# A two-layer graph network on one core: TensorE gets six products on constants behind each pair of build products of the first layer

## The chip, the cores and the metric

The kernel runs on 1 core of one Trainium2 chip. The metric is device time in microseconds (us); lower is better. Three runs of the kernel before took 5845.89, 5846.42 and 5848.63 us, median 5846.42 us.

## What is computed

There are 12500 nodes with 32 features and 400000 edges, sorted by destination. The first layer gathers the source's row for each edge, adds the edge's features, takes the relu and sums over each destination; then comes a layer norm with a residual. The second layer gathers, sums and scales by the square roots of both degrees, and there is a second layer norm. Cut to what matters:

```python
def _L0_gnn_ref(node_feat, edge_feat, eps, src, dst):
    m = jax.nn.relu(node_feat[src] + edge_feat)
    neigh = jax.ops.segment_sum(m, dst, num_segments=node_feat.shape[0])
    return (1.0 + eps[0]) * node_feat + neigh

def _L1_gnn_ref(node_f, src, dst):
    out_deg = jnp.clip(jax.ops.segment_sum(ones, src, num_segments=n), 1.0)
    in_deg = jnp.clip(jax.ops.segment_sum(ones, dst, num_segments=n), 1.0)
    x = node_f * jax.lax.rsqrt(out_deg)[:, None]
    agg = jax.ops.segment_sum(x[src], dst, num_segments=n)
    return agg * jax.lax.rsqrt(in_deg)[:, None]

x = _layernorm(x + _L0_gnn_ref(x, edge_attr_32, L0_gnn_eps, src, dst), axis=-1)
x = _layernorm(x + _L1_gnn_ref(x, src, dst), axis=-1)
```

## The kernel before

The edges are cut into G = 125 groups of 3200 edges (128 partitions x J = 25). The first layer (`layer_0`) handles one group per **turn**. The function `turns` writes turns 0 to 3 out, runs turns 4 to 119 in a loop of 29 passes with four turns each, and writes out turns 120 to 126. Each engine has its own program of `step(g, slot, u)`, and semaphores alone tie them together.

- **GpSimd (POOL)** issues the 25 row gathers of turn g (L166), into one of four buffers `rows`. Ahead of the first it waits until the sums of step g - 1 are done:

```python
gp.wait_ge(z_agg, g - 1)
gathers(gp, 0, J, x[:, :], rows[:, slot, :, :], src_t[:, slot, :], z_rows[slot])
```

- **VectorE (DVE)** works one turn behind. In step g it waits for the rows of turn g - 1 and adds them to the edge features (`add(0)`, L427), makes the parts of `msg` and the one-hot matrix `hot`, takes the sums of the step before out of PSUM (`sums_out`, L467 and L468), and makes one-hot matrices `b_hot` and `key_hot` for the build products, in three chunks a turn.
- **TensorE (PE)** makes two kinds of products in step g. The **build products** (L708) are 12 pairs, n = 0 to 11, into the two PSUM buffers `built[n % 2]`; they count edges per pair of nodes, and the second layer uses the counts. The **sums** (`sum_up`, L688) are 25 products of `msg` with `hot` into one bank; they aggregate the messages of turn g - 1. Three sums stand behind pair 9, three behind pair 10 and 19 behind pair 11; the last one raises `z_agg`. A small product (`fold_sums`, L676) stands ahead of pair 8. Pair n waits until ScalarE has copied pair n - 2 out of PSUM.
- **ScalarE (ACT)** copies each pair to `stage`, a part of the tile `big` (`evict`, L642). Between these copies stand its six steps on messages, L620, L627 and L631. The copy of pair 1 stands behind `first_part(0)` (L627), which waits for `add(0)`.
- **SyncE (SP)** loads indices and edge features, and stores `stage` to memory once a turn.

`spare` in the change is the identity matrix `ident`, 128x128 in float32, seen as 128x256 numbers in bf16. `fold_bank` is the PSUM bank of L676, which uses its partitions 0 to 32; the new products write its partitions 64 to 127.

The second layer (`layer_1`) follows behind a barrier. It has no gathers in its main loop: it applies the stored counts with products of 160 columns (L1082).

Of the kernel before, what the change touches and what calls it, by code (L numbers as in the profile page):

```python
# [4 lines left out]
F32, BF16, F16, I32, U32 = mybir.dt.float32, mybir.dt.bfloat16, mybir.dt.float16, mybir.dt.int32, mybir.dt.uint32  # L5
# [4 lines left out]
P = 128  # L10
# [6 lines left out]
def build(nc, x, src, dst, edge, eps, out, table, x1):  # L17
# [47 lines left out]
    with ExitStack() as ctx:  # L65
# [15 lines left out]
        ident = sb("ident", [P, P])  # L81
# [11 lines left out]
        A1 = 64  # L93
# [128 lines left out]
        def layer_0():  # L222
# [5 lines left out]
            def turns(engine, step):  # L228
                for g in range(4):
                    step(g, g, 0)  # L230
                with engine.Fori(0, fours) as i:
                    for slot in range(4):
                        step(i * 4 + (4 + slot), slot, i + 1)
                for g in range(4 + 4 * fours, G + 2):
                    step(g, g % 4, g // 4)

            def builds(g):

                return not isinstance(g, int) or g < G

            def sends(g):

                return not isinstance(g, int) or 1 <= g <= G

            def adds(g):

                return not isinstance(g, int) or 2 <= g
# [12 lines left out]
            with ExitStack() as own:  # L260
# [112 lines left out]
                def prepare_pe(te):  # L373
                    te.wait_ge(s_v, n_first)
                    PE(te.transpose(misc[0:JT, 0:NC], c_first[:, :], ident[0:NC, 0:NC]))
                    te.wait_ge(s_v, n_keys)
                    for k, (what, t, m) in enumerate(ROUNDS):
                        if k >= 2:
                            te.wait_ge(s_a, k - 1)
                        for q in range(m):  # L380
                            turned = (c_hi, c_key)[what][:, t + q, :]
                            last = te.transpose(turn[k % 2][0:TP, q * NC:(q + 1) * NC], turned, ident[0:NC, 0:NC])
                        PE(last)
                    te.wait_ge(s_v, n_base)
                    PE(te.matmul(spread[:, 0:G], ones_row[:, :], first[0:1, :], start=True, stop=True))
                    te.wait_ge(s_v, n_bad)
                    for h in range(2):
                        te.matmul(misc[0:HS[h], h * NC:(h + 1) * NC], pick[:, h, 0:HS[h]], first[:, :], start=True, stop=True)
                    PE(te.matmul(misc[0:1, 2 * NC:2 * NC + 1], bad[:, :], ones[0:NC, :], start=True, stop=True))
# [8 lines left out]
                with nc.Block() as block:  # L398
# [266 lines left out]
                    @block.tensor  # L665
                    def _(te):
                        te.wait_ge(s_v, n_const)
                        prepare_pe(te)

                        def step(g, slot, u):  # L670
                            def fold_sums():

                                if adds(g):

                                    te.wait_ge(z_taken, g - 1)
                                    te.matmul(folded, fold_r[:, :], taken[:, :], start=True, stop=True).then_inc(z_folded, 1)  # L676

                            def sum_up(j0, j1):

                                if not sends(g):  # L680
                                    return
                                for j in range(j0, j1):
                                    if j == 0:

                                        te.wait_ge(z_hot, g)
                                    if j == JA:
                                        te.wait_ge(z_part2[1], g)
                                    last = te.matmul(agg_bank[:, :], msg[:, j, :], hot[:, j, :], start=(j == 0), stop=(j == J - 1))  # L688
                                if j1 == J:
                                    last.then_inc(z_agg, 1)  # L690

                            if not builds(g):
                                fold_sums()
                                sum_up(0, J)
                                return
                            for n in range(BP):
                                if n == 2 * CP:
                                    fold_sums()
                                r = (slot * HB + n // CP) % 2
                                if n % CP == 0:  # L700
                                    te.wait_ge(z_chunk[n // CP], g + 1)
                                if n >= 2:
                                    te.wait_ge(z_counts[n - 2], g + 1)
                                elif not (isinstance(g, int) and g == 0):
                                    te.wait_ge(z_counts[BP + n - 2], g)
                                for b in range(2):
                                    t = n % CP * 2 + b
                                    last = te.matmul(built[n % 2][:, b, 0:KEYS], b_hot[:, r, t, :], key_hot[:, r, t, :], start=True, stop=True)  # L708
                                last.then_inc(z_built[n], 1)
                                if n >= BP - 3:  # L710

                                    sum_up((n - BP + 3) * 3, (n - BP + 4) * 3)
                            sum_up(9, J)
                        turns(te, step)

                general_sums(0, x[:, :], J, DE, (src_t, dst_t, rows, quot, hot[:, :, 0:W], agg_bank[:, 0:W]), edge_t, msg[:, :, X:R], msg[:, :, 0:1])
# [643 lines left out]
```

## Time and profile before

| | value |
|---|---|
| median of three runs | 5846.42 us |
| span of the profiled execution, first to last instruction | 5163.0 us |
| its own time | not given beside its span; the median less the span is 683.4 us |
| first layer, first gather to last sum | 9.3 us to about 3936 us |
| second layer, from there to the end | about 1227 us |
| mean granted TensorE clock over the span | 0.735 |

### The profile page before, as it was taken

The numbers are of one execution on the slowest core, as the hardware profiler recorded it, in microseconds if no ns is written. First come the engines' busy times: TensorE is split into PE (matmuls) and PEld (weight loads), VectorE is DVE, ScalarE is ACT, GpSimd is POOL, SyncE is SP. The second block draws the span as 40 slices with busy tenths as digits, with TensorE's granted clock in tenths as the row PEclk, the third lists the DMA queues.
The fourth block names the chain that finished last, engine by engine and source line by source line (L and its number), as shares of the span: only waits on it lengthen the run. The fifth ranks groups of instructions, "written<-read, shape, count | busy, mean of one in ns | idle before, by whom it ended". The sixth has DMA issues, their size and how long they took to land. (4 is left out here: it accounts for less than half of the span.)

```text
span 5163.0 us, 62751 instructions
## 1 busy us (share of the span) xinstructions
PE 3304.6 (64%) x21148; PEld 1672.0 (32%) x21148; DVE 3278.0 (63%) x4723; ACT 2748.4 (53%) x2907; POOL 2960.2 (57%) x3134
## 2 busy tenths in 40 slices
PE   4555555555555555555555555555555999999998
PEld 1111111111111111111111111111113888888887
DVE  7766666666666666666666666666666444444444
ACT  4555555555555555555555555555554555555554
POOL 7777777777777777777777777777772000000000
PEclk8666666666666666666666666666666999999998
DMA  3333333333333333333333333333334999999996
GB/s 126 120 120 134 129 120 120 120 120 126 126 134 123 120 120 120 120 122 135 126 120 120 120 121 126 128 134 120 120 117 168 327 328 326 326 326 326 327 327 232
DMA packets 269133, 867.70 MB, mean 168 GB/s; under 512 B 90218, under 2 KB 140218, under 8 KB 252602
## 3 DMA queue, kind: packets, MB, share of 16 engines
q1 hardware_dynamic: 169107, 815.98, 42.5%
q0 software_dynamic: 100000, 51.40, 6.1%
q8 instruction: 13, 0.21, 0.0%
q14 instruction: 13, 0.11, 0.0%
HBM read 486.77 MB, written 380.38 MB: 168 GB/s over the span
## 5 line engine op out<-in xcount | busy, mean ns | idle before, releaser
L166 POOL DMA_INDIRECT rows<-in_x,src_t x3125 | 2958.5, 947 | 959.1 <-issue 946.9
L708 PE MATMUL built<-x_parts,b_hot 100*128 100x490 bf16 x3000 | 1289.6, 533 | 1757.8 <-ACT big L642 1743.4
L642 ACT ACTIVATE big<-built 128x980 bf16<-128x980 f32 x1500 | 1803.2, 1228 | 542.7 <-PE built L708 539.1
L708 PEld LDWEIGHTS built<-x_parts,b_hot 100*128 100x128 bf16 x3000 | 248.8, 111 | 2644.1 <-ACT big L642 2025.7
L1082 PE MATMUL applied<-counts,x_parts 128*96 128x160 bf16 x12250 | 915.9, 233 | 18.1 <-DVE x_parts L894 18.1
L427 DVE TENSOR_TENSOR sum_ps<-sum_ps,rows 128x416 f32<-128x416 f32 x250 | 142.9, 572 | 1210.9 <-DMA rows<-in_x,src_t 1205.7
L688 PE MATMUL agg<-hot,msg 128*128 128x512 bf16 x3125 | 899.2, 438 | 11.4 <-DVE msg L457 11.4
L1082 PEld LDWEIGHTS applied<-counts,x_parts 128*96 128x96 bf16 x12250 | 880.0, 123 | 79.4 <-issue 19.4
L146 DVE TENSOR_TENSOR x_parts<-iota_ps,hk_g 100x3920 bf16<-100x3920 f16 x375 | 819.4, 2185 | 0.0
L1038 ACT ACTIVATE counts<-built 128x980 bf16<-128x980 f32 x496 | 594.7, 1240 | 386.8 <-PE built L1065 386.8
L146 DVE TENSOR_TENSOR hot<-iota_ps,s_hi 128x5252 bf16<-128x5252 f16 x250 | 691.3, 2765 | 0.0
L627 ACT ACTIVATE msg<-sum_ps 128x416 bf16<-128x416 f32 x250 | 122.8, 491 | 793.6 <-DVE sum_ps L427 793.6
L688 PEld LDWEIGHTS agg<-hot,msg 128*128 128x128 bf16 x3125 | 351.1, 112 | 511.9 <-issue 240.6
L631 ACT ACTIVATE msg<-sum_ps 128x416 bf16<-128x416 f32 x250 | 125.9, 504 | 383.7 <-DVE sum_ps L432 383.7
L146 DVE TENSOR_TENSOR big<-iota_ps,hk_g 100x3920 bf16<-100x3920 f16 x125 | 273.6, 2189 | 0.0
L1065 PE MATMUL built<-big,hi_hot 100*128 100x490 bf16 x992 | 269.0, 372 | 0.8 <-DVE big L146 0.8
L146 DVE TENSOR_TENSOR b_hot<-iota_ps,hk_g 100x1024 bf16<-100x1024 f16 x375 | 255.1, 680 | 7.9 <-PE built L708 3.6
L1005 DVE CAST slots<-small 80x64 bf16<-80x64 f32 x125 | 27.6, 221 | 355.0 <-PE small L1093 355.0
L146 DVE TENSOR_TENSOR hot<-iota_ps,rel 128x1404 bf16<-128x1404 f16 x250 | 209.7, 839 | 0.0
L620 ACT ACTIVATE sum_ps<-edge_t 128x416 f32<-128x416 f32 x250 | 126.9, 508 | 68.6 <-DVE msg L436 68.6
L1019 DVE TENSOR_TENSOR acc<-acc,small 32x108 f32 x125 | 33.2, 266 | 200.0 <-PE small L1103 200.0
L432 DVE SCALAR_TENSOR_TENSOR sum_ps<-sum_ps,msg 128x416 f32<-128x416 f32 x250 | 141.5, 566 | 3.7 <-ACT msg L627 3.7
(132 smaller groups left out, 1425.0 us busy)
## 6 DMA issues: line engine op xcount, KB each, us to landing
stash<-big SPq DMA_DIRECT2D x125, 2940.0 KB
counts<-stash SPq DMA_DIRECT2D x250, 1470.0 KB, 8.7
rows<-in_x,src_t POOLq DMA_INDIRECT x3125
edge_t<-in_edge_attr SPq DMA_DIRECT2D x61, 800.0 KB
big<-in_dst SPq DMA_DIRECT2D x1, 1562.5 KB
big<-in_src SPq DMA_DIRECT2D x1, 1562.5 KB
src_t<-in_src SPq DMA_DIRECT2D x61, 24.8 KB
dst_t<-in_dst SPq DMA_DIRECT2D x61, 24.8 KB
```

Source lines behind the costliest of these rows:

```text
L146: return ve.tensor_tensor(out.rearrange("p n (w t) -> p n w t", t=2), row[0:p, 0:w].rearrange("p (w t) -> p w t", t=2).unsqueeze(1).to_bro ...
L166: gp.indirect_dma_start(rows_d[:, j, :], None, nodes, bass.IndirectOffsetOnAxis(ap=src_d[:, j:j + 1].bitcast(U32), axis=0),).then_inc(s, 16)
L427: ve.tensor_tensor(half(h), half(h), rows[:, prev, j0:j1, :], ALU.add).then_inc(z_sum[h], 1)
L432: ve.scalar_tensor_tensor(half(h), half(h), 0.0, part(0, h), ALU.max, ALU.subtract).then_inc(z_left[h], 1)
L620: sc.activation(half(h), edge_t[:, prev, j0:j1, :], ACT.Copy).then_inc(z_copy[h], 1)
L631: sc.activation(part(1, h), half(h), ACT.Copy).then_inc(z_part1[h], 1)
L642: sc.activation(stage[:, slot % 2, q, :, d0:d0 + 2 * SPAN].rearrange("p c (b d) -> p b c d", b=2), built[n % 2][:, :, 0:KEYS].rearrange("p ...
L688: last = te.matmul(agg_bank[:, :], msg[:, j, :], hot[:, j, :], start=(j == 0), stop=(j == J - 1))
L708: last = te.matmul(built[n % 2][:, b, 0:KEYS], b_hot[:, r, t, :], key_hot[:, r, t, :], start=True, stop=True)
L1038: sc.activation(counts[:, slot, HB, :, d0:d0 + 2 * SPAN].rearrange("p c (b d) -> p b c d", b=2), built[n % 2][:, :, 0:KEYS].rearrange("p b ...
L1065: last = te.matmul(built[n % 2][:, b, 0:KEYS], hi_hot[:, slot, t, :], key_hot[:, slot, t, :], start=True, stop=True)
L1082: last = te.matmul(applied[slot].rearrange("m (q d) -> m q d", d=CS), x_parts[:, c, :], counts[:, other, :, c, :], start=(c == 0), stop=(c ...
```

## The change

TensorE's program of the first layer gets a helper that makes n products of the same constants, 64 output partitions by 256 columns. It is called with n = 6 behind each of the 12 pairs of build products of a turn, and behind the last sum. Nothing reads the result, and nothing waits for these products but what stands behind them in TensorE's own program.

```diff
                         prepare_pe(te)
 
+                        spare = ident[:, :].bitcast(BF16)
+
+                        def idle_products(n):
+                            for _ in range(n):
+                                te.matmul(fold_bank[A1:P, 0:256], spare[:, 0:P - A1], spare[:, :], start=True, stop=True)
+
...
                                 if j1 == J:
                                     last.then_inc(z_agg, 1)
+                                    idle_products(6)
...
                                 last.then_inc(z_built[n], 1)
+                                idle_products(6)
                                 if n >= BP - 3:
 
                                     sum_up((n - BP + 3) * 3, (n - BP + 4) * 3)
```

The first place is the end of a turn on TensorE, inside the loop. These are the rows of the kernel before, from the build products of pairs 8 and 9 to the 19 last sums:

```order
L708 MATMUL built<-x_parts,b_hot 128x490 x4
L688 MATMUL agg<-hot,msg 128x512 x3
L708 MATMUL built<-x_parts,b_hot 128x490 x2
L688 MATMUL agg<-hot,msg 128x512 x3
L708 MATMUL built<-x_parts,b_hot 128x490 x2
L688 MATMUL agg<-hot,msg 128x512 x19
```

The same stretch in the changed kernel, where L715 is the build product, L674 the new one and L694 the sum:

```order
L715 MATMUL built<-x_parts,b_hot 128x490 x2
L674 MATMUL fold_bank<-ident 64x256 x6
L715 MATMUL built<-x_parts,b_hot 128x490 x2
L674 MATMUL fold_bank<-ident 64x256 x6
L694 MATMUL agg<-hot,msg 128x512 x3
L715 MATMUL built<-x_parts,b_hot 128x490 x2
L674 MATMUL fold_bank<-ident 64x256 x6
L694 MATMUL agg<-hot,msg 128x512 x3
L715 MATMUL built<-x_parts,b_hot 128x490 x2
L674 MATMUL fold_bank<-ident 64x256 x6
L694 MATMUL agg<-hot,msg 128x512 x19
L674 MATMUL fold_bank<-ident 64x256 x6
```

Of the new products of a turn, 18 stand between the pairs 9 to 11 and the sums that follow them, six stand behind the last sum, and the other 54 stand behind the pairs 0 to 8. No other row of TensorE moves, and the programs of the other engines are unchanged.

## Rows read from the trace of the kernel before

**Rows 1.** The page: busy tenths, clock and DMA in 40 slices of the span.

```profile
POOL 7777777777777777777777777777772000000000
PEclk8666666666666666666666666666666999999998
```

**Rows 2.** Groups of instructions between 2000 and 3000 us (busy, mean; idle before).

```profile
L166 POOL DMA_INDIRECT rows<-in_x,src_t x801 | 755.9, 944 | 244.1 <-issue 242.9 <-PE agg L688 1.2
L642 ACT ACTIVATE big<-built 128x980 bf16<-128x980 f32 x385 | 462.9, 1228 | 138.8 <-PE built L708 138.2
```

**Rows 3.** Who waited for whom between 2000 and 3000 us: total, times, longest.

```profile
PE built L708 <- ACT big L642: 457.4, 192, 8.2
DVE sum_ps L427 <- DMA rows<-in_x,src_t: 320.1, 32, 10.4
```

**Rows 4.** The waits of POOL between 0 and 260 us.

```profile
POOL rows L166 <- PE agg L688: 3.3, 2, 3.0
```

**Rows 5.** Timeline of POOL: the gather that waited, and the last turn's first and last.

```profile
146.15 0.94 POOL L166 DMA_INDIRECT rows<-in_x,src_t  x1 [2.96 <-PE agg L688]
...
3891.63 0.94 POOL L166 DMA_INDIRECT rows<-in_x,src_t  x1 [0.30 <-issue]
...
3921.59 0.94 POOL L166 DMA_INDIRECT rows<-in_x,src_t  x1 [0.30 <-issue]
```

**Rows 6.** Timeline of PE: sums of step 3, then pairs 3 to 11 and sums of step 123.

```profile
141.07 4.26 PE L688 MATMUL agg<-hot,msg 128*128 128x512 bf16 x19
...
3864.29 1.00 PE L708 MATMUL built<-x_parts,b_hot 100*128 100x490 bf16 x2 [7.29 <-ACT big L642]
3867.58 2.05 PE L708 MATMUL built<-x_parts,b_hot 100*128 100x490 bf16 x4 [2.29 <-ACT big L642]
...
3876.61 1.00 PE L708 MATMUL built<-x_parts,b_hot 100*128 100x490 bf16 x2 [2.09 <-ACT big L642]
3877.40 1.49 PE L688 MATMUL agg<-hot,msg 128*128 128x512 bf16 x3
3878.68 1.02 PE L708 MATMUL built<-x_parts,b_hot 100*128 100x490 bf16 x2
...
3881.34 4.26 PE L688 MATMUL agg<-hot,msg 128*128 128x512 bf16 x19
```

**Rows 7.** Windows: busy time of PE, PEld, DVE, ACT, POOL; clock; DMA share, GB/s.

```profile
61.40:75.00 13.60, 11.55 (x24) 1.71 (x24) 8.32 (x7) 12.38 (x11) 10.25 (x12) 0.50 0.10 13
3876.60:3881.00 4.40, 4.39 (x11) 1.63 (x12) 4.32 (x9) 3.44 (x3) 3.43 (x4) 0.50 0.10 15
3881.10:3891.20 10.10, 5.93 (x27) 2.36 (x25) 2.02 (x1) 2.94 (x3) 7.66 (x9) 1.00 0.77 304
3943.00:3955.00 12.00, 12.00 (x83) 9.41 (x82) 9.18 (x16) 3.48 (x3) 0.00 (x0) 0.50 0.10 11
```

**Rows 8.** Timeline of PE: transposes against the identity matrix, before the first turn.

```profile
45.05 3.33 PE L382 MATMUL built<-ident,x_parts 125*100 125x125 f32 x16 [22.50 <-DVE big L354]
48.55 1.14 PE L382 MATMUL built<-ident,x_parts 125*100 125x125 f32 x8 [0.17 <-ACT hk_all L607]
```

**Rows 9.** Timeline: products of 160 columns in the second layer; ACT in step 123.

```profile
4000.34 1.89 PE L1082 MATMUL applied<-counts,x_parts 128*96 128x160 bf16 x25
...
3875.29 3.55 ACT L642 ACTIVATE big<-built 128x980 bf16<-128x980 f32 x3
```

**Rows 10.** Timeline of all engines around the last rows' landing; then DVE in step 123.

```profile
3924.46 0.52 DVE L457 TENSOR_TENSOR msg<-iota_ps,s_lo 128x372 bf16<-128x372 f16 x1
3924.91 0.58 DVE L427 TENSOR_TENSOR sum_ps<-sum_ps,rows 128x416 f32<-128x416 f32 x1
...
3862.00 0.60 DVE L427 TENSOR_TENSOR sum_ps<-sum_ps,rows 128x416 f32<-128x416 f32 x1 [10.19 <-DMA rows<-in_x,src_t]
```

**Rows 11.** DMA queues that carry code, and two issues (KB each, us to landing).

```profile
q8 instruction: 13, 0.21, 0.0%
q14 instruction: 13, 0.11, 0.0%
...
counts<-stash SPq DMA_DIRECT2D x250, 1470.0 KB, 8.7
...
edge_t<-in_edge_attr SPq DMA_DIRECT2D x3, 400.0 KB, 3.4
```

## The prediction

> **What bounds the kernel now.** I read the page's slices first. In the first 30 of 40 slices POOL is steady at 7 tenths and TensorE's clock is 0.6; behind that POOL is nearly empty and the clock is near full [rows 1]. Seven tenths is not idle time: in the groups of a stretch of 1000 us, 801 gathers keep POOL busy for 755.9 us, and of the 244.1 us between them 242.9 are "issue", the 0.30 us that stand ahead of every gather whatever else happens [rows 2]. So a gather costs 1000/801 = 1.248 us and a turn 25 x 1.248 = 31.2 us. The timeline shows that this holds everywhere. Turn 4 begins at 146.15 and the last gather, the 3025th from there on, at 3921.59 [rows 5]: 3775.44 us for 3024 steps, 1.2485 us each. From 146 us on POOL waits for nobody, and the first layer lasts as long as its gathers.
>
> The waits show the reverse side. VectorE waits for rows in each of 32 turns, up to 10.4 us and 320.1 us in all, and TensorE waits 457.4 us in 1000 for ScalarE's copies [rows 3]. TensorE is late for nobody as long as `z_agg` comes before POOL needs it.
>
> How much room is there? In step 123 the last 19 sums start at 3881.34 and end at 3885.60 [rows 6]; the first gather that waits for them starts at 3891.63 [rows 5]. Where POOL really waited, the sums ended at 141.07 + 4.26 = 145.33 [rows 6] and the gather began at 146.15 [rows 5], 0.8 us later. So the room is 3891.63 - 0.8 - 3885.6 = 5.2 us. A delay beyond it is not paid whole. Gathers of turn g wait for the sums of step g - 1, and the sums of step g + 1 wait for those gathers, so the ring takes two turns: a delay of e behind the sums costs (e - 5.2)/2 a turn.
>
> **What the change costs on TensorE.** The trace has no product of 64x256. Sums of 512 columns follow each other at (3878.68 - 3877.40)/3 = 0.427 us at the low clock and 4.26/19 = 0.224 us at the high one [rows 6]; half the columns gives 0.213 and 0.11 us. From the other side, 25 products of 160 columns take 1.89 us at the high clock, 0.076 us each [rows 9]; by columns that is 0.12 us. I take 0.213 and 0.11: six cost 1.28 us low and 0.66 us high, and their weight loads lie under the product before, as those of the sums do. A pair of build products takes 0.79 us low (3877.40 - 3876.61) [rows 6], about 0.42 high. With its six it takes 2.07 or 1.08 us; ScalarE copies a pair in 3.55/3 = 1.18 us [rows 9]. At the high clock ScalarE stays the slower one, at the low clock TensorE becomes it. A turn's 78 new products are 16.6 us low or 8.6 us high.
>
> So all hangs on the clock. In the window from 3876.60 to 3881.00 TensorE was busy 4.39 of 4.40 us at 0.50, and in the next window it has 1.00 [rows 7]. From 61.40 to 75.00 it was busy only 11.55 of 13.60 us, with build products alone, and the clock stayed at 0.50 [rows 7]. With the new products it has no gap there.
>
> I walk step 123 with the clock rising some 4.4 us after the dense stretch begins. Pair 3 starts at 3864.29, as now, since it waits for rows. Pair 4 waits for its copy until 3867.58, ends with its six at 3869.7; pair 5 ends at 3871.8; there the clock is high. Pairs 6 and 7 end at 3872.9 and 3874.0, the fold and pair 8 at 3875.4. Pair 9 waits for the copy of pair 7 until 3876.6, as now. Then come three pairs with their sixes (3 x 1.08), six sums (1.3) and 19 sums (4.26): 3885.4 us, against 3885.6. The sums come when they came, and POOL notices nothing: **0 us** for turns 4 to 124. What is faster on TensorE is added to its idle time, and what is slower is taken from it.
>
> Beside the row stands the Trainium skill, page "TensorE: Matmul & The Clock Gate", section "Why this matters for your kernels": keep TensorE busy without a break, and the clock stays at its full rate. By that rule the sums and builds halve. By the groups above this still takes nothing from 1.2485 us a gather, so the sum by rule and row is the same, 0.
>
> **Where TensorE does stand on the path.** (a) The start. POOL's only long wait is 2.96 us for the sums of step 3 [rows 4, 5]; steps 0 to 3 run as fast as VectorE, ScalarE and TensorE allow, the gathers being ahead. In step 0 pair 1 comes 1.28 us late behind the first six at the low clock, later pairs keep ScalarE's pace. At the end of steps 1 to 3, six products stand ahead of pair 0 (0.66 us each); against that, the pairs that ScalarE waits for come up to 0.4 us earlier. Bounds: -2.7 us (the wait is gone, 2.96 less the usual 0.30) and 1.3 + 3 x 1.1 = +4.6 us; I take +2. (b) The end. In step 125 VectorE reaches the last rows at 3924.91, with L457 ending just then (3924.46 + 0.52) [rows 10], so sums of step 124 that come late push it; by the walk they come at -0.2, and I take 0 with a bound of +2. The six behind the last sum lie under VectorE's copy that the fold waits for. The second layer has none of the new products, and the 683.4 us outside the span stay. Sum: 5163.0 + 2 + 683.4, about 5848.4 us.
>
> **Rivals.** *1, the clock rises only with the sums.* The low clock isn't left for every busy stretch: from 3943 to 3955 narrow transposes kept TensorE busy 12.00 of 12.00 us at 0.50 [rows 7]. The new products use half the output partitions and operands that are nearly all zeros. For the rise speaks that transposes against the same identity matrix went from 3.33/16 = 0.208 to 1.14/8 = 0.143 us each within one burst [rows 8]. The Trainium skill has a rule against that in the same page, section "Part 4: PE-mode transpose": transposes don't count as busy for the gate; in this trace those of rows 8 did end in the high clock, the narrow ones didn't. In this case pair 9 begins at 3867.58 + 5 x 2.07 + 0.6 for the fold = 3878.5, and the clock rises 4.4 us behind that, at 3882.9. Pair 9 and three sums end at 3881.9, pair 10, partly at the high clock, at 3883.4, three sums and pair 11 at 3885.1, the 19 sums at 3889.4: 3.8 us late, inside the 5.2. The loop costs nothing, but the start does: step 0 runs 12 pairs at 2.07 instead of 1.18 (+10 us), and steps 1 to 3 lose 3 to 4 us each, like the 3.8 above. Together +12 to +25, about 5866 us. Chance 0.16.
>
> *2, the constants hold the clock down until the 19 sums, the case on the other side.* Pairs, sixes and the first six sums low: pair 9 begins at 3878.5, pair 11 with its six ends 3 x 2.07 + 6 x 0.427 later, at 3887.3. With a rise 4.4 us into the 19 sums (10 low, 9 high) these end at 3893.6: 8.0 us late, (8.0 - 5.2)/2 = 1.4 us a turn, 168 us over 120 turns; all low 9.8 us late, 276 us. With 25 to 30 us at the start: +193 to +306, about 6090 us. It decides from 5.2 us late on. It needs the clock not to answer to TensorE being full, which rows 7 and 8 speak against. Chance 0.08.
>
> *3, code.* The loop's four turns hold 4 x 50 = 200 products before and 4 x 128 = 512 now, each with a weight load. Before, neither code queue moved more than 13 packets for 29 passes [rows 11], so the loop was not fetched again. If a longer one is, the nearest landings are 3.4 and 8.7 us [rows 11]. Once a pass, at the branch behind the sums, this falls into 7 us of idle TensorE and costs 0; once a turn ahead of the sums, (8.7 - 5.2)/2 x 120 = 210 us at most. The Trainium skill, page "Runtime: NRT & Kernel Launch", section "Instruction fetch mechanics", says that a taken branch to code that is no longer held forces such a fetch, and gives TensorE's store as 2048 instructions; the new loop is by that an estimated 1050. Chance 0.04.
>
> *4, faster by over 0.2%* (11.7 us, about what a measurement can tell from no change): the gathers would have to get cheaper, and the start gives 2.7 us at most. Chance 0.03.
>
> **How the numbers follow.** My forecast, the clock high from early in each dense stretch, has 0.66 and its own range 5842 to 5856. With 1, 2, 3, 4 and 0.03 for what I don't see that is 1. The range 5841 to 5880 holds the forecast and rival 1, 0.82. Same: 0.66 and a fifth of rival 1 and half of 3, 0.71. Slower: the rest of 1, 2, half of 3, the unseen, 0.25. Faster: 0.04.
>
> **What would show it.** Right: POOL 801 gathers per 1000 us and no wait for L694 beyond 0.3; clock near 0.8 to 1.0 instead of 0.66 over the first layer; the six in about 1.3 and 0.66 us; ScalarE's waits for build products shorter; the gather of turn 4 between 143.5 and 151 us; as many code packets per pass as before, none. Wrong: the clock at 0.5 between 61 and 80 us and in pairs 3 to 9 (rival 1); POOL waiting 1.5 us or more per turn for the sums (2); code packets in the loop (3); or a time outside the span other than 683 us.

## The result, and the profile after

The changed kernel takes **7469.98 us** (four runs, 7464.41 to 7477.74) beside 5846.16 us (5844.13 to 5848.63): the ratio is 1.2778, with a 95% interval from 1.276 to 1.2796. It is 28% slower. The forecast was 5848.4 us.

The page of the changed kernel answers to [rows 1] and the table: the span, the slices of POOL and of the clock, and the costliest groups of POOL, ScalarE and the new products.

```profile
span 7463.6 us, 82126 instructions
...
POOL 5344454444544454444544454444544451000000
PEclk7777677766777667776777667766777677999999
...
L166 POOL DMA_INDIRECT rows<-in_x,src_t x3125 | 2957.5, 946 | 3238.0 <-PE agg L694 2318.3
L642 ACT ACTIVATE big<-built 128x980 bf16<-128x980 f32 x1500 | 1810.5, 1231 | 4072.3 <-remote 2567.9
```

Two things stand there. A gather costs what it cost (946 ns), but POOL now waits 2318.3 us in all for the sums, where it had waited 1.2 us in a stretch of 1000 [rows 2]. And the time less the span is 7465.73 - 7463.6 = 2.1 us for the profiled run, where for the kernel before I had 683.4 us.

The waits between 2000 and 3000 us answer to [rows 3]:

```profile
ACT big L642 <- remote: 463.5, 57, 17.1
...
POOL rows L166 <- PE agg L694: 368.5, 20, 19.2
PE built L715 <- ACT big L642: 304.4, 37, 16.3
```

POOL waits 18.4 us in each of 20 turns. ScalarE waits up to 17.1 us for something the profile calls "remote": it finds no instruction that ended just then. The timeline of one turn shows what that is. The last gather of the turn is at 2051.41, the next turn's first at 2070.38.

```profile
2021.44 0.95 POOL L166 DMA_INDIRECT rows<-in_x,src_t  x1 [18.78 <-PE agg L694]
...
2027.80 0.59 PE L715 MATMUL built<-x_parts,b_hot 100*128 100x490 bf16 x2
...
2029.92 0.59 PE L715 MATMUL built<-x_parts,b_hot 100*128 100x490 bf16 x2 [0.76 <-issue]
...
2037.18 1.19 ACT L642 ACTIVATE big<-built 128x980 bf16<-128x980 f32 x1 [6.93 <-remote]
...
2051.41 0.94 POOL L166 DMA_INDIRECT rows<-in_x,src_t  x1 [0.31 <-issue]
2054.74 1.19 ACT L642 ACTIVATE big<-built 128x980 bf16<-128x980 f32 x1 [16.04 <-remote]
...
2065.29 4.27 PE L694 MATMUL agg<-hot,msg 128*128 128x512 bf16 x19
...
2070.38 0.94 POOL L166 DMA_INDIRECT rows<-in_x,src_t  x1 [18.02 <-PE agg L694]
```

TensorE ends pair 5 at 2028.4 and pair 6 at 2030.5 (the two build rows). ScalarE copies pair 5 at 2037.18, after 6.93 us of idleness, and pair 6 at 2054.74, after 16.04 us. By the profile the work is done, but **the signal that it is done arrives 9 and 24 us late**. In this turn the second one comes 2.4 us after POOL's last gather ended (2051.41 + 0.94 = 2052.35). Only then does the turn go on: 15 us of pairs and sums until 2069.6, and the next gathers. So this turn is 30.9 us of gathers, 2.4 us, and 15.6 us of what should have run under them: 48.9 us instead of 31.2.

In the trace's records of semaphores, beside the modelled ends of the products that raise them, this reads as follows, in us. Some records are missing, so only products with one record each are told. The kernel before is here its trace ahead of the prediction, which is of another kind of chip, as the experiments will show.

```
product that signals        kernel before       changed kernel
pair 7, L708 / L715         0.014               0.014 to 22.8, median 19.1
fold, L676 / L682           0.014               0.014 to 22.3, median 18.2
last sum, L688 / L694       0.014               0.014
second layer's products     0.014               0.014
```

Three things stand in these records of the changed kernel. Only TensorE's signals are late: from the fifth turn to the 119th, 607 of its 1450 records lie over 0.3 us behind the work, and none of ScalarE's 1446 or VectorE's 1362 (of which three in ten are missing, though). Each turn begins on time: the signals of pairs 0 to 2 come after 0.014 us, though gathers are in flight. And a late signal isn't held until the gathers pause: over 108 turns, pair 5's 81 recorded signals all came while gathers still ran, and so did 38 of pair 6's 93. What was left came out after them: pair 7's and the fold's signals 4.5 and 4.6 us (medians) behind the end of the turn's last gather, every time.

The same trace holds the other half. POOL waits for the sums from about 143 to 243 us, so no gather is issued, and there steps 2 and 3 of the changed kernel run undisturbed: the 19 sums of steps 1, 2 and 3 start at 188.01, 213.81 and 238.04 us, 24 to 26 us apart, and the signals of the pairs come after 0.014 us.

```profile
243.12 0.94 POOL L166 DMA_INDIRECT rows<-in_x,src_t  x1 [99.97 <-PE agg L694]
```

### The profile page after: what moved, and what is told of

It is laid out like the page before. It is cut to its first block and busy times, and to the rows that moved or that the text cites. A ratio compares the mean times of both kernels' runs of the same rounds, so it can differ in the third digit from the quotient of the medians.

```text
span 7463.6 us, 82126 instructions
## 1 busy us (share of the span) xinstructions
PE 4427.6 (59%) x30773; PEld 2606.7 (35%) x30898; DVE 3333.9 (45%) x4723; ACT 2716.0 (36%) x2907; POOL 2959.2 (40%) x3134
## 5 line engine op out<-in xcount | busy, mean ns | idle before, releaser
L166 POOL DMA_INDIRECT rows<-in_x,src_t x3125 | 2957.5, 946 | 3238.0 <-PE agg L694 2318.3
L715 PE MATMUL built<-x_parts,b_hot 100*128 100x490 bf16 x3000 | 1060.2, 441 | 2891.2 <-ACT big L642 1750.2
L674 PE MATMUL fold_bank<-ident 128*64 128x256 bf16 x9750 | 1638.7, 313 | 0.0
L674 PEld LDWEIGHTS fold_bank<-ident 128*64 128x64 bf16 x9750 | 1063.8, 123 | 897.7 <-issue 835.9
L715 PEld LDWEIGHTS built<-x_parts,b_hot 100*128 100x128 bf16 x3000 | 206.6, 103 | 3301.3 <-issue 2530.8
L694 PE MATMUL agg<-hot,msg 128*128 128x512 bf16 x3000 | 757.3, 397 | 50.2 <-issue 38.8
L436 DVE TENSOR_TENSOR msg<-sum_ps,msg 128x416 bf16<-128x416 f32 x250 | 142.2, 569 | 1316.7 <-ACT msg L631 1019.9
L694 PEld LDWEIGHTS agg<-hot,msg 128*128 128x128 bf16 x3125 | 283.3, 101 | 414.6 <-issue 137.9
L521 DVE TENSOR_TENSOR acc<-acc,fold_bank 33x108 f32 x125 | 32.4, 259 | 416.0 <-remote 406.4
```

The source lines that it names most:

```text
L166: gp.indirect_dma_start(rows_d[:, j, :], None, nodes, bass.IndirectOffsetOnAxis(ap=src_d[:, j:j + 1].bitcast(U32), axis=0),).then_inc(s, 16)
L436: ve.tensor_tensor(part(2, h), half(h), part(1, h), ALU.subtract).then_inc(z_part2[h], 1)
L674: te.matmul(fold_bank[A1:P, 0:256], spare[:, 0:P - A1], spare[:, :], start=True, stop=True)
```

## The experiments

Each row of a run's record gives a time and a span; all differ by some 2 us. Chips are told apart by the kernel before on them: **5167 us (first kind, two chips)** or **5847 to 5854 us (second kind, three chips)**. The trace ahead of the prediction, with its span of 5163.0 us, is one of the first kind, and the three times beside it are of the second. Only one chip, of the first kind, was used on two occasions, so whether a kind belongs to the chip or to its condition at the time is not told apart; "kind of chip" stands for either.

| kernel | first kind, us | second kind, us |
|---|---|---|
| before | 5166.9, 5166.9, 5166.4 | 5846.9, 5846.8, 5848.1, 5853.75 |
| six products of 256 columns (the change) | 5176.5 | 7472.6, 7480.3 |
| three of 256 | 5178.9, 5178.4, 5180.2 | 6738.8 |
| three of 512 | 5171.8, 5172.2 | 7026.0 |
| six of 64 | 5176.6, 5176.6 | 7205.0 |
| six, behind the last sum alone | 5168.3 | |
| twelve of 256 | | 8393.0 |
| six of 256, no gathers | | 4368.5 |

All are single runs but 5853.75 (seven) and 7480.3 (four).

**Three products, sums alone, wide and narrow ones.** The edits of the first four runs, each against the changed kernel:

```diff
-                                    idle_products(6)
+                                    idle_products(3)
...
-                                idle_products(6)
+                                idle_products(3)
```

> Three constant products instead of six at each place. In the changed kernel the work of TensorE is done early, but what it signals to ScalarE (the end of a build pair) arrives up to 38 us late while gathers are in flight. Theory A (each product instruction issued while gathers are in flight adds to that lateness): about half of the added 1620 us, 6500 to 6800 us. Theory B (a threshold or a state of the whole run, not the number of products): near 7460 or near 5850 us, nothing between. Theory C (TensorE's time itself is on the path): 5850 us, because half of the time of six, 4.3 us a turn at the high clock, fits into the room.

For the sums alone the call behind the build pairs is taken out:

```diff
                                 last.then_inc(z_built[n], 1)
-                                idle_products(6)
```

> Only the six products behind the last sum of a turn stay; the 72 behind the build pairs are gone. Theory A: 6 of 78 products, about +125 us or less, 5850 to 5970 us. Theory B (state): 7460 or 5850 us. Theory C: 5846 us.

The wide ones: three calls instead of six, and

```diff
-te.matmul(fold_bank[A1:P, 0:256], spare[:, 0:P - A1], spare[:, :], start=True, stop=True)
+te.matmul(fold_bank[A1:P, 0:512].rearrange("p (a c) -> p a c", a=2), spare[:, 0:P - A1], spare[:, :].unsqueeze(1).to_broadcast([P, 2, 256]), start=True, stop=True)
```

> Three products of 512 columns instead of six of 256: TensorE's time is as in the changed kernel, the number of product instructions is half. Theory A (number of instructions): as with three products of 256 columns, 6500 to 6800 us. Theory C (TensorE's time or its activity): as in the changed kernel, about 7465 us.

The narrow ones:

```diff
-te.matmul(fold_bank[A1:P, 0:256], spare[:, 0:P - A1], spare[:, :], start=True, stop=True)
+te.matmul(fold_bank[A1:P, 0:64], spare[:, 0:P - A1], spare[:, 0:64], start=True, stop=True)
```

> Six products of 64 columns instead of 256: as many instructions as in the changed kernel, a quarter of the columns. Theory A (number of instructions): about 7465 us or more, since they come closer together. Theory C (TensorE's time or activity): 5850 to 6250 us.

Measured: 5178.93, 5168.26, 5171.76 and 5176.64 us, beside **5166.94 us for the kernel before**. None of the theories was tested, since the kernel before had lost its 680 us as well. That was the find: from one chip to another, a kernel that hasn't changed differs by 13%.

**The changed kernel again, and twelve products.** The second is the changed kernel with `idle_products(12)` in both places.

> The changed kernel once more, beside a kernel before that takes 5167 us on this chip and not 5846. Theory D (the 5846 and the 7470 us belong to a condition of the chip or session in which TensorE's signals are late while gathers are in flight, in both kernels): 5170 to 5200 us. Theory E (six products of 256 columns pass a threshold that three, or six narrow ones, do not pass): about 7465 us here too, beside 5167.

> Twelve products instead of six at each place: 156 a turn, 17.2 us at the high clock, so 28 us of TensorE's 31.2 us a turn are used. Theory D: TensorE's time decides, and the sums come some 4 us later than with six, 5180 to 5350 us. Theory E: above the changed kernel, 8500 us or more.

Measured: 7480.3 us beside 5853.75 us, ratio 1.278 (1.2758 to 1.2801), and 8393.01 us. This was another chip, of the second kind, so D and E weren't told apart yet. Twelve add 8393.0 - 7480.3 = 913 us to six, 7.5 us in each of 121 turns: less than theory E's 8500 us and far above theory D's 5350 us.

**The first four once more, for the other kind of chip.**

> The kernel before, for its trace on a chip where it takes about 5850 us. Theory D (late signals of TensorE while gathers are in flight, on some chips): there its build pairs of the middle of a turn are seen by ScalarE microseconds late, POOL waits for the sums some 5.5 us a turn, and 121 turns of 36.8 instead of 31.2 us make the 683 us. On a chip where it takes 5167 us: no such waits.

> Three products of 256 columns at each place, 39 a turn. On a chip where the kernel before takes 5167 us: 5179 us as measured. Where it takes about 5850 us: theory A (lateness grows with the number of product instructions) 6550 to 6800 us; theory C (with TensorE's time) the same.

> Three products of 512 columns, as many instructions as with three narrow ones and as much TensorE time as in the changed kernel. Chip at 5167: 5172 us. Chip at 5850: theory A as three products of 256 columns, 6550 to 6800 us; theory C about 7470 us.

> Six products of 64 columns, as many instructions as in the changed kernel and a quarter of the columns. Chip at 5167: 5177 us. Chip at 5850: theory A about 7470 us; theory C 6000 to 6300 us.

Measured: 5166.42, 5178.4, 5172.23 and 5176.55 us. It was the chip of the first four again; each repeats its first time within 0.6 us.

**The second kind of chip, with a trace of the kernel before, and without gathers.** The edit of the third run leaves the 3125 row gathers out and loads fixed rows, once a turn, so it computes something else:

```diff
-gathers(gp, 0, J, x[:, :], rows[:, slot, :, :], src_t[:, slot, :], z_rows[slot])
+gp.dma_start(rows[:, slot, :, :].rearrange("p j d -> p (j d)"),
+             x[0:P * J, :].rearrange("(p j) d -> p (j d)", p=P)).then_inc(z_rows[slot], 16)
...
-ve.wait_ge(z_rows[prev], loads(slot, u) * (16 * J))
+ve.wait_ge(z_rows[prev], loads(slot, u) * 16)
```

> The changed kernel a third time, so far only measured where the kernel before takes 5850 us. If this chip takes 5167 us for the kernel before: theory D (a condition of the chip) 5170 to 5200 us; theory E (a threshold of the kernel's own) about 7470 us. If it takes 5850 us: 7470 us, and the runs below are read against it.

> The kernel before, for its trace. Theory D, where it takes 5850 us: pairs of the middle of a turn seen late by ScalarE while gathers are in flight, POOL waiting about 5.5 us a turn for the sums, fewer records of gather landings. Where it takes 5167 us: 5166 us and no such waits, as before.

> The changed kernel without its 3125 row gathers; one plain transfer a turn brings fixed rows, so the result is not that of the reference. TensorE's work and the new products are unchanged. Theory D (lateness needs gathers in flight): turns of 22 to 26 us as between 160 and 250 us of the changed kernel's trace, 4100 to 4500 us on either chip. Theory F (the new products make TensorE's signals late whatever else runs): above 6000 us where the changed kernel takes 7470.

> Six products of 64 columns instead of 256. Chip at 5167: 5177 us. Chip at 5850: theory A (lateness grows with the number of product instructions) about 7470 us; theory C (with TensorE's time) 6000 to 6300 us.

Measured: 7472.58, 5848.07, 4368.48 and 7205.01 us. These four settle most. First the **kernel before** on this kind of chip. The waits of POOL over the whole span answer to [rows 4]:

```profile
POOL rows L166 <- issue: 915.6, 3003, 0.3
POOL rows L166 <- remote: 620.0, 120, 5.6
POOL rows L166 <- PE agg L688: 84.1, 1, 84.1
```

620.0 us in 120 turns, 5.2 us each, and 84.1 us once, at the start: 704.1, of which the usual 0.30 us for each of 121 gathers is 36. That leaves 668 of the 681.7 us between the two spans (5846.0 less 5164.3). The timeline of one turn end, to lay beside [rows 5, 6]:

```profile
2019.88 4.94 PE L688 MATMUL agg<-hot,msg 128*128 128x512 bf16 x19
...
2029.53 0.94 POOL L166 DMA_INDIRECT rows<-in_x,src_t  x1 [0.30 <-issue]
...
2034.93 1.26 ACT L642 ACTIVATE big<-built 128x980 bf16<-128x980 f32 x1 [3.44 <-remote]
2035.66 0.95 POOL L166 DMA_INDIRECT rows<-in_x,src_t  x1 [5.18 <-remote]
```

The sums end at 2024.82, 5.6 us before the last gather ends (2030.47). The record of their signal lies at 2034.86, and POOL goes on at 2035.66: the lateness was in the kernel before, on this kind of chip. Over the layer the last sum's signal is late by 12.7 us (median; 14.7 at most) and comes 4.4 us after the end of the turn's last gather. Pairs 2 to 9 are on time where they are recorded; pair 11, ahead of the 19 sums, is late by 9.1 us, and pair 0, behind them, by 12.3 us (medians).

It needs no full TensorE either. At the start, with gathers going out and build products alone, TensorE is busy 8.67 of 39 us, and ScalarE waits for each pair:

```profile
105.00:144.00 39.00, 8.67 (x18) 1.25 (x17) 5.46 (x5) 8.55 (x7) 29.55 (x32) 0.50 0.10 13
```

```profile
108.38 1.00 PE L708 MATMUL built<-x_parts,b_hot 100*128 100x490 bf16 x2 [1.67 <-issue]
113.92 1.00 PE L708 MATMUL built<-x_parts,b_hot 100*128 100x490 bf16 x2 [4.54 <-ACT big L642]
```

```profile
112.67 1.19 ACT L642 ACTIVATE big<-built 128x980 bf16<-128x980 f32 x1 [4.34 <-remote]
117.57 1.19 ACT L642 ACTIVATE big<-built 128x980 bf16<-128x980 f32 x1 [3.71 <-remote]
```

The pair that starts at 108.38 ends at 109.38 and is copied at 117.57. These are the turns behind POOL's one wait of 84.1 us.

Second, the changed kernel **without gathers** on the same chip: 4368 us against 7473. Its waits between 2000 and 3000 us and its windows:

```profile
ACT big L643 <- PE built L716: 244.9, 122, 4.6
```

```profile
1000.00:2000.00 1000.00, 902.09 (x5214) 460.31 (x5255) 857.85 (x1102) 659.97 (x734) 22.00 (x41) 0.99 0.43 158
```

No "remote" wait is left; all 1500 pairs are signalled 0.014 us after their end. The 78 new products a turn are there, the clock is 0.99 and TensorE is busy 902 us of 1000. So the new products alone hold nothing back, and theory F falls. The 5255 weight loads in 1000 us, one for each of 128 products a turn, are 41 turns of 24.4 us, as theory D expected. Lateness needs gathers in flight **and** this kind of chip; how much TensorE does decides how many of a turn's signals it catches. That a plain transfer a turn replaces 25 indirect ones changes their kind and their number together; which of the two matters isn't told apart.

Third, six narrow products lose 11.2 us a turn, where six of 256 columns lose 13.4. That is neither theory A's 7470 us nor theory C's 6000 to 6300.

**The changed kernel on the first kind of chip.**

> The changed kernel, hoped for on a chip where the kernel before takes 5167 us. Theory D there: 5175 to 5200 us, every pair of build products seen by ScalarE at once, the clock above 0.9 in the first layer. Theory E (the kernel's own threshold): 7470 us. On a chip at 5850: 7470 us again.

> Three products of 256 columns, 39 a turn. Chip at 5167: 5179 us, as measured twice. Chip at 5850: signals of TensorE pile up while gathers are in flight and come out when these pause, so a turn is 31.2 us of gathers, 2.4 us of landing and then what is left of the turn behind the first held signal. With six products the held signal is that of pair 5 or 6 (49.0 us a turn); with three it should be of a later pair, 8 or 9, with 8 to 12 us left: 42 to 46 us a turn, 6500 to 6950 us. If the number of products doesn't matter for it: 7400 us and more.

Measured: **5176.52 us** beside 5166.93 us, and 5180.21 us. Theory E falls: the same program takes 5177 us on one chip and 7473 us on another. Its waits of POOL over the span, and a window that answers to the one at 61.40 in [rows 7], with one of the steady loop:

```profile
POOL rows L166 <- issue: 951.4, 3122, 0.3
POOL rows L166 <- PE agg L694: 9.5, 2, 9.2
```

```profile
61.40:75.00 13.60, 13.16 (x66) 6.26 (x66) 7.11 (x8) 9.78 (x8) 10.25 (x12) 0.80 0.10 14
1000.00:2000.00 1000.00, 808.05 (x4130) 390.03 (x4130) 675.99 (x865) 538.07 (x577) 755.91 (x802) 0.84 0.36 123
```

POOL waits once, 9.2 us at the start, and 802 gathers fit into 1000 us as before. The clock is 0.84 instead of 0.66, below the 0.9 that I had expected. All of TensorE's signals are on time (at most 0.25 us for the fold, 0.014 us for the rest). With three products the first window stays at the low clock:

```profile
61.40:75.00 13.60, 13.21 (x39) 3.83 (x40) 6.11 (x7) 8.79 (x8) 10.25 (x12) 0.50 0.08 14
```

**Three products on the second kind of chip.**

> Three products of 256 columns, 39 a turn. Chip at 5167: 5180 us, as measured three times. Chip at 5850: signals pile up while gathers are in flight and come out when these pause; with three products the first held signal should be of a later pair (8 or 9 instead of 5 or 6), 42 to 46 us a turn, 6500 to 6950 us. If the number of products doesn't matter: 7400 us and more.

> Three products of 512 columns, as many instructions as in the run with three of 256 and as much of TensorE's time as in the changed kernel. Chip at 5167: 5172 us. Chip at 5850: if the number of instructions decides, within 3% of the run with three of 256 columns; if TensorE's time decides, near 7470 us.

Measured: 6738.8 and 7026.01 us beside 5846.84 us. Of the kernel with three of 256 columns, waits of POOL and ScalarE in one turn:

```profile
2020.18 0.95 POOL L166 DMA_INDIRECT rows<-in_x,src_t  x1 [0.30 <-issue]
2023.64 1.26 ACT L642 ACTIVATE big<-built 128x980 bf16<-128x980 f32 x1 [17.64 <-remote]
...
2034.18 0.94 POOL L166 DMA_INDIRECT rows<-in_x,src_t  x1 [13.06 <-PE agg L694]
```

In this turn the pair that comes out behind the last gather is pair 8 instead of 6, and what is left of the turn behind it is 10.5 us instead of 15.6, as expected (42 to 46 us a turn; a gather every 1000/586 = 1.706 us makes 42.7). The expectation's rule of a signal held until the gathers pause is too simple here too: 66 of pair 8's 85 recorded signals came while gathers ran. Pair 10's came 4.45 us (median) after the last gather. The expectation for the wide ones wasn't met cleanly: 4.3% above the three of 256, where 3% was the bound. Against the kernel before on the same kind of chip, in us for each of 121 turns, rounded:

| added a turn | products | columns | lost, us a turn |
|---|---|---|---|
| three of 256 | 39 | 9984 | 7.4 |
| three of 512 | 39 | 19968 | 9.7 |
| six of 64 | 78 | 4992 | 11.2 |
| six of 256 | 78 | 19968 | 13.4 |

Twice the products at the same columns costs 3.7 us more; twice the columns at the same products costs 2.4, and four times 2.2. Half the columns in twice the products loses 3.8 us more. So the number of products counts most here, and their time counts too. Each of the four is a single run.

## Why the prediction was wrong

**The step that failed** is the term of the loop, "The sums come when they came, and POOL notices nothing: **0 us** for turns 4 to 124". On the chips that the times come from it measured **13.4 us a turn**, (7469.98 - 5846.16)/121, which is the whole miss. The term was read from a trace of the other kind of chip, and the sum's last term hid that: "the 683.4 us outside the span stay". They weren't outside any span. Every run since lies within some 2 us of its own span. 683 of 5846 us, 13% more than the page could explain, was the plain sign that trace and times came from different conditions, and I carried it along as a constant. Spread over 121 turns it is 5.6 us a turn, more than the 5.2 us of room that I had just worked out for the sums. That would not have given the 13.4 us, but it would have warned that something already cost time in each turn that the trace didn't show.

**"TensorE is late for nobody"** and "POOL waits for nobody" hold on the first kind of chip alone. On the second, POOL already waited 5.2 us a turn for the sums before the change, so the room was used up.

**The form of the loss.** Rival 2 had the place (the sums come too late for POOL) but the wrong cause, the clock, and a price of 1.4 to 2.3 us a turn with a lateness at most 4.6 us beyond the room. Measured are 13.4 us a turn more than before. Its halving rule doesn't apply either: the signals of pair 7 and of the fold come out some 4.5 us after the last gather, so the rest of the turn's products stands behind the gathers, every turn.

**What was right, on the first kind of chip.** The loop: from the gather of turn 4 to the last one there are 3776.8 us (153.44 to 3930.20) against 3775.4, nothing to speak of. The clock rose, to 0.80 in the window from 61.40. Rival 1 fell for six products; with three its start did show (0.50 in that window, and 5178.4 to 5180.2 us, 11.5 to 13.3 us above the kernel before, where rival 1 had +12 to +25). The Trainium skill's advice to keep TensorE busy (page "TensorE: Matmul & The Clock Gate", section "Why this matters for your kernels") held as far as the clock, and its faster products bought nothing in time, as the rows said. **The start was mis-sized**: I took +2 us, at most +4.6, and the gather of turn 4 came at 153.44 instead of 146.15, +7.3 us (+6.1 beside the other trace of the kernel before on this kind, which has 147.35). The timeline of that run shows why:

```profile
68.02 0.59 PE L715 MATMUL built<-x_parts,b_hot 100*128 100x490 bf16 x2
68.54 0.84 PE L674 MATMUL fold_bank<-ident 128*64 128x256 bf16 x6
69.31 0.59 PE L715 MATMUL built<-x_parts,b_hot 100*128 100x490 bf16 x2
```

A pair and its six take 69.31 - 68.02 = 1.29 us at the high clock, not 1.08: in that trace a new product starts 0.302 us after the last build product, where build products follow each other at 0.216 us, and the next build product 0.205 us after the last new one, where new ones follow at 0.109 us. So TensorE, not ScalarE with 1.18 us, can set the pace of steps 0 to 3; 48 pairs at 0.11 us would be 5.3 of the 7.3 us, an estimate that no run tests. In all the change costs 9.6 us on this kind of chip, 0.19%.

**Rival 3, code**, fell. Over the whole run one code queue moved 21 packets instead of 13 [rows 11], fewer than the loop's 29 passes; the rule of the Trainium skill (page "Runtime: NRT & Kernel Launch", section "Instruction fetch mechanics") wasn't put to work, since the longer loop was not fetched again.

```profile
q8 instruction: 21, 0.34, 0.0%
```

**What stays open** is what holds the signals back. Shown are the two conditions, that of the recorded signals TensorE's alone are late, and that those left over come out 4.4 to 4.6 us after a turn's last gather. The ends of products are modelled, so that the product itself is done in time rests on the starts of those behind it. In the traces of the second kind most records of the gathers' own landings are missing as well: for one of the four row buffers there are 12,718 in the kernel before's first trace, 3,047 in its trace on the other kind, 2,043 in the changed kernel's; three products on the first kind have 12,748. So a path for such events may be full on these chips, and the recording of the profile may be a part of the load: every time here, the timed runs' too, has a recorded span. No run was made without it, so whether the 7470 us would stand without it is not known.

## What to carry to other kernels

Before anything is predicted, lay the time beside the span of the trace: if they differ by more than some microseconds, the trace is of another condition, and the difference divided by the number of turns tells how much each turn of it may lack. A change is compared on one chip only, and a kernel in which TensorE signals to others while an engine issues gathers is measured on more than one. Products that only keep the clock up are not free where another engine waits for TensorE's signals: here they bought 0.84 instead of 0.66 of the clock, and no time on any chip used.

## What the runs showed of the hardware that I had not expected

- The same program takes 5167 us on some chips and 5847 us on others, and another 5177 and 7473 us; the one chip that was used twice repeated its four times within 0.6 us.
- With gathers in flight, TensorE's signals reach ScalarE and POOL microseconds after the work on the slower chips: in the changed kernel up to 27 us in the loop and 38 us at the start, with TensorE busy a fifth of the time as well (the kernel before, 105 to 144 us). ScalarE's and VectorE's recorded signals are on time.
- Three products of 512 columns behind each pair cost less at the start (5172 us) than three of 256 (5178 to 5180 us) on the first kind of chip. In the window from 61.40 to 75.00 the clock is 0.50 with three of 256 columns and with six of 64, though TensorE is busy 13.2 and 13.3 of 13.6 us by the profile.

```profile
61.40:75.00 13.60, 13.33 (x74) 4.88 (x74) 8.30 (x8) 11.00 (x9) 10.25 (x12) 0.50 0.09 14
```
